# A softmax weighting moved behind the rotated rows of its chunk, and the last layer's norm moved from VectorE to ScalarE, in a two-layer audio tower

## The reference

```
h = layernorm(layernorm(patches(x)) @ W + b)                       # 64 sequences of 23 rows, 512 wide
h = h + power_attention(layernorm(h))                              # layer 0
h = h + shared_expert(layernorm(h)) + top4_of_16_experts(...)
h = h + softmax(rope(Q) rope(K)^T / sqrt(32), causal) V Wo         # layer 1, 16 heads, 4 of keys and values, from layernorm(h)
h = h + down(silu(gate(z)) * up(z)),  z = layernorm(h)
      # gate, up, down: x -> int8 rows of rmsnorm(x) (scale 127 / max|x| per row), ternary weights
```

## Time and profile before

| | |
|---|---|
| median of three runs | 1389.83 us |
| the profiled execution | 1393.95 us, of which its span 1391.8 us |
| TensorE busy | 1228.5 us (88%) |
| VectorE busy | 864.6 us (62%) |
| ScalarE busy | 613.2 us (44%) |
| mean granted TensorE clock | 0.939 of full speed |

### The profile page before, as it was taken

How to read it: one execution, slowest core, us unless ns; L and a number is a source line. 1 busy time by engine, 2 the same in 40 slices (tenths; PEclk the granted TensorE clock), 3 DMA queues, 4 the chain that set the end, 5 groups by cost and what they waited for, 6 DMA issues and landing times.

```text
span 1391.8 us, 30551 instructions
## 1 busy us (share of the span) xinstructions
PE 1228.5 (88%) x10764; PEld 718.6 (52%) x10778; DVE 864.6 (62%) x1767; ACT 613.2 (44%) x1054; POOL 231.8 (17%) x280
## 2 busy tenths in 40 slices
PE   5999899999999999957799999999957885959997
PEld 2447566666666666635344444444524664424443
DVE  5985454655546555488844454554357677778886
ACT  3444444544445444425244444444423332246664
POOL 2220000000000000000123333333258600110000
PEclk9997999999999999986999999999977887989998
DMA  5121452444524435214147767775247700000000
GB/s 196 61 83 49 154 202 109 181 175 162 198 109 181 181 145 210 107 46 185 46 150 251 265 218 279 262 253 183 92 129 135 105 7 2 1 1 16 23 23 27
DMA packets 43277, 180.98 MB, mean 130 GB/s; under 512 B 9172, under 2 KB 10512, under 8 KB 35408
## 3 DMA queue, kind: packets, MB, share of 16 engines
q0 software_dynamic: 19744, 95.41, 20.7%
q1 hardware_dynamic: 20016, 72.15, 14.6%
q10 hardware_dynamic: 3456, 12.58, 2.5%
HBM read 132.39 MB, written 47.73 MB: 129 GB/s over the span
## 4 chain that ended last, share of the span: by engine, by line
PE 52%; DVE 24%; issue 13%; ACT 4%; POOL 2%; DMA 2%; DVEq 1%; another core or an unknown queue 0%; SPq 0%; ACTq 0%; POOLq 0%
PE ps L935 14%; PE ps L937 13%; PE ps L936 13%; DVE rs L1611 2%; PE ps L1049 2%; DVE ff L2043 2%; DVE amf L2050 2%; PE ps L1028 1%; PE ps L1123 1%; PE ps L1376 1%; DVE we_sp L1405 1%; DVE bst L1478 1%; PE ps L1264 1%; ACT vp L682 1%; PE ps L1358 1%
## 5 line engine op out<-in xcount | busy, mean ns | idle before, releaser
L935 PE MATMUL ps<-nT_hi,wa_hi 128*128 128x368 f16 x576 | 189.2, 328 | 11.8 <-DVE wa_lo L1405 7.7
L936 PE MATMUL ps<-nT_lo,wa_hi 128*128 128x368 f16 x576 | 188.8, 328 | 0.0
L937 PE MATMUL ps<-nT_hi,wa_lo 128*128 128x368 f16 x576 | 188.1, 327 | 0.0
L1772 DVE SCALAR_TENSOR_TENSOR nrm<-ps,xg,nrm 128x256 f32<-128x256 f32 x61 | 29.5, 483 | 122.9 <-ACT nrm L749 103.1
L523 POOL DMA_INDIRECT xg<-xrow,idx x61 | 61.2, 1004 | 263.4 <-PE ps L1123 113.8
L935 PE MATMUL ps<-wide,xT 128*128 x244 | 92.7, 380 | 13.8 <-issue 9.3
L1605 DVE SCALAR_TENSOR_TENSOR a<-sq,eps_row,E 128x184 f32<-128x184 f32 x32 | 13.1, 409 | 131.3 <-ACT sq L699 131.3
L1579 DVE SCALAR_TENSOR_TENSOR wide<-ps,wide 128x368 f32<-128x368 f32 x128 | 66.8, 537 | 42.0 <-PE ps L937 42.0
L936 PE MATMUL ps<-wide,xT 128*128 x244 | 92.5, 379 | 0.0
L937 PE MATMUL ps<-wide,xT 128*128 x244 | 92.5, 379 | 0.0
L1358 PE MATMUL ps<-qw,qT 128*128 128x512 bf16 x372 | 85.6, 383 | 4.0 <-DVE ff L2043 2.6
(11 more groups left out here) (317 smaller groups left out, 2893.6 us busy)
## 6 DMA issues: line engine op xcount, KB each, us to landing
we_st<-in_we POOLq DMA_DIRECT2D x16, 1536.0 KB, 6.8
wsp<-we_sp POOLq DMA_DIRECT2D x16, 1536.0 KB, 5.4
wide<-wsp SPq DMA_DIRECT2D x16, 1536.0 KB
yslot<-yt POOLq DMA_DIRECT2D x61, 256.0 KB
wq_st<-in_ffq SPq DMA_DIRECT2D x24, 512.0 KB, 4.5
wq_st<-in_ffq ACTq DMA_DIRECT2D x24, 512.0 KB, 3.5
wide<-in_wa SPq DMA_DIRECT2D x10, 1024.0 KB, 6.9
xt<-in_x SPq DMA_DIRECT2D x12, 512.0 KB, 3.5
```

The costliest lines, as they stand in the source:

```text
L935: nc.tensor.matmul(dst, lhs[0], rhs[0], start=start, stop=False)
L936: nc.tensor.matmul(dst, lhs[0], rhs[1], start=False, stop=False)
L937: return nc.tensor.matmul(dst, lhs[1], rhs[0], start=False, stop=stop)
L1772: V.scalar_tensor_tensor(ht, ps[:, 2 + p, FI:2 * FI], AS / WS if x is None else xgw[:, x, ds(D + e, 1)], sgt[:, p, :], ALU.mult, ALU.mult) ...
```

## The change

1. In chunk c, VectorE does `weights(c-1)` behind all rotations, `rotated(c)` and the low halves of the next rows, just ahead of `centred(c)`. `group_stats(c+1)` goes between `rotate(c, 0)` and `rotate(c, 1)`, `group_shift(c+1)` behind `rotate(c, 1)`, and `low(k)` behind `rotate(c, 3)`.
2. TensorE does `turn(c-1)` behind `project(c+1, 0)` and `(c+1, 1)`, just ahead of `weighted(c-1)`. The two row turns and `scores(c)` follow `project(c, 5)` directly. ScalarE does `weights_turned(c-1)` behind `moved(c+1, 1)`, ahead of `exponential(c)`.
3. The last layer's norm is one ACTIVATE on ScalarE (bias and scale per row, `f_norm`); VectorE only writes the bias (`f_shift`, one column). The turn on VectorE is now `w_add(n)`, `f_shift(n-2)`, `largest(n-3)`, `w_moments(n-1)`, and is written out instead of looped.
4. The first scales are taken of four rows (turns 6 and 7) instead of eight, and the integers of rows 0 and 1 are written in turns 8 and 9, amid the output rows. The scales of the other eight are asked for behind the last row and worked out behind turn 3 of the last pipeline.
5. TensorE does `q_turn(0)` between `out_rows(10)` and `out_rows(11)`; ScalarE does `f_turned_rows(0)` behind the square of row 9; the first `gate_up` waits for all of `w_add`.

```
# POOL
-            pipeline(pool, NT, [(0, lambda k, p, half: root(rf_ask, k, rt_in[:, p:p + 1], rt_out[:, p:p + 1], rf_done))])
-            for n, x in enumerate((slice(0, EARLY), slice(EARLY, NT))):
-                root(rq_ask, n, rq_in[:, x], rq_out[:, x], rq_done)
+            for k in range(NT):
+                if k == FIRST + 2:                                   # FIRST = 4
+                    root(rq_ask, 0, rq_in[:, 0:FIRST], rq_out[:, 0:FIRST], rq_done)
+                root(rf_ask, k, rt_in[:, k % 2:k % 2 + 1], rt_out[:, k % 2:k % 2 + 1], rf_done)
+            root(rq_ask, 1, rq_in[:, FIRST:NT], rq_out[:, FIRST:NT], rq_done)
# ScalarE, attention
                 moved(c, 5)
-                if c:
-                    weights_turned(c - 1)
                 ...
                     moved(c + 1, 0)
                     moved(c + 1, 1)
+                if c:
+                    weights_turned(c - 1)
                 exponential(c)
# ScalarE, rows
+            def f_norm(k):
+                act.wait_ge(w_nb, k + 1)
+                nc.scalar.activation(xn[:, k, :], h[:, k, :], ACT.Identity, bias=nb12[:, k % 2:k % 2 + 1],
+                                     scale=rt_out[:, k % 2:k % 2 + 1]).then_inc(w_n, 1)
-            pipeline(act, NT, [(0, f_square)])
+            for k in range(NT):
+                f_norm(k)
+                f_square(k)
+                if k == NT - 3:
+                    f_turned_rows(0, 0, 0)
# TensorE
-                if c:
-                    turn(c - 1, k if inner else NT - 1)
                 if inner:
-                    for j in (k + 1, k + 2):
-                        pe.wait_ge(f_pe, ready(4 * (c - 1) + 2 + j % 2))
-                        row_turn_l1(j)
+                    row_turn_l1(k + 1)
+                    row_turn_l1(k + 2)
                 ...
                 scores(c)
                 if c + 1 < CH:
                     project(c + 1, 0)
                     project(c + 1, 1)
                 if c:
+                    turn(c - 1, k + 2 if inner else NT - 1)
                     weighted(c - 1)
-            for k in range(NT):
+            for k in range(NT - 1):
                 out_rows(k, k % 2, k // 2)
             def gate_up(k, fs):
                 if fs[0] == 0:
+                    if type(k) is int and k == 0:
+                        pe.wait_ge(w_h, ready(NT - 1))
                     pe.wait_ge(w_ev, k + 2)
                 ...
-                              (1, lambda k, p, half: gate_up(k, (2, 3))), (2, f_turn)])
+                              (1, lambda k, p, half: gate_up(k, (2, 3))), (2, f_turn)],
+                     after={0: lambda: out_rows(NT - 1, (NT - 1) % 2, (NT - 1) // 2)})
# VectorE, attention: the new order
+                rotate(c, 0)
+                if inner: group_stats(c + 1)
+                rotate(c, 1)
                 ...                                                  # y_low(c - 2) as before
+                if inner: group_shift(c + 1)
+                rotate(c, 2); rotate(c, 3)
+                if inner: low(k)
+                rotate(c, 4); rotated(c)
+                if inner: low(k + 1); low(k + 2)
+                if c: weights(c - 1)
                 centred(c)
# VectorE, rows
+            def f_shift(k, p, half):
+                dve.wait_ge(rf_done, k + 1)
+                V.scalar_tensor_tensor(nb12[:, p:p + 1], mv12[:, p, 0:1], -1.0, rt_out[:, p:p + 1], ALU.mult, ALU.mult).then_inc(w_nb, 1)
-            pipeline(dve, NT, [(0, w_add), (2, f_norm), (1, w_moments), (3, largest)], order, 2,
-                     after={NT: lambda: ask_rows(0, EARLY), NT + 1: lambda: row_scales(0, 0, EARLY)})
-            ask_rows(EARLY, NT)
+            for n in range(NT + 3):
+                for lag, step in ((0, w_add), (2, f_shift), (3, largest), (1, w_moments)):
+                    if 0 <= n - lag < NT:
+                        step(n - lag, (n - lag) % 2, 0)
+                if n == FIRST + 2:
+                    ask_rows(0, FIRST)
+                if n == FIRST + 3:
+                    row_scales(0, 0, FIRST)
+                if 0 <= n - NT + 4 < AHEAD:                          # AHEAD = 2
+                    quantize(n - NT + 4, 0, 0)
+                    integers(n - NT + 4, 0, 0)
+            ask_rows(FIRST, NT)
...
-                     order, 1 + 2 + 4 + 2, after={1: lambda: row_scales(1, EARLY, NT)})
+                     order, 1 + 2 + 4 + 2, after={3: lambda: row_scales(1, FIRST, NT)})
```

More of the change, by code:

```diff
@@ L40 @@
 EARLY = 8
+FIRST = 4
+AHEAD = 2
 GT = 3
@@ L363, in build @@
         f_pt, f_pe, f_av, f_hi, f_lo = sems("f", "pt pe av hi lo")
-        w_mm, w_h, w_n, w_sq, w_am, w_r, w_q, w_tr, w_ev = sems("w", "mm h n sq am r q tr ev")
+        w_mm, w_h, w_nb, w_n, w_sq, w_am, w_r, w_q, w_tr, w_ev = sems("w", "mm h nb n sq am r q tr ev")
         x_gu, x_dq, x_sg, x_t, x_sq, x_am, x_q, x_tr, x_ev, x_dn, x_og = sems("x", "gu dq sg t sq am q tr ev dn og")
@@ L867, in _, with f_square @@
             y_high(CH - 1)
-            def f_square(k, p, half):
+            def f_norm(k):
+                act.wait_ge(w_nb, k + 1)
+                nc.scalar.activation(xn[:, k, :], h[:, k, :], ACT.Identity, bias=nb12[:, k % 2:k % 2 + 1],
+                                     scale=rt_out[:, k % 2:k % 2 + 1]).then_inc(w_n, 1)
+            def f_square(k):
                 act.wait_ge(w_n, k + 1)
                 act.wait_ge(w_sq, k + 1)
-                nc.scalar.activation(jk, xn[:, ds(k, 1), :].rearrange("p a b -> p (a b)"), ACT.Square,
-                                     accum_out=Gm["ssq"][:, ds(k, 1)]).then_inc(w_sq, 1)
+                nc.scalar.activation(jk, xn[:, k, :], ACT.Square, accum_out=Gm["ssq"][:, k:k + 1]).then_inc(w_sq, 1)
             def f_turned_rows(k, p, half):
@@ L910, in f_turned, with f_turned_next @@
                                          ps[:, 4 + j, :].bitcast(BF16), ACT.Copy).then_inc(x_ev, 1)
-            pipeline(act, NT, [(0, f_turned_rows), (1, gated), (2, f_turned)])
+            def f_turned_next(k, p, half):
+                if type(k) is not int or k > 0:
+                    f_turned_rows(k, p, half)
+            pipeline(act, NT, [(0, f_turned_next), (1, gated), (2, f_turned)])
         @block.tensor
@@ L1947, in _ @@
                 k = GT * (c + 1)
+                inner = 0 < c < CH - 1
                 rotate(c, 0)
+                if inner:
+                    group_stats(c + 1)
                 rotate(c, 1)
@@ L1955, in _ @@
                     y_low(c - 2)
-                if c:
-                    if c + 1 < CH:
-                        group_stats(c + 1)
-                        group_shift(c + 1)
-                    weights(c - 1)
-                for j in range(2, 5):
-                    rotate(c, j)
-                    if j == 2 and 0 < c < CH - 1:
-                        low(k)
+                if inner:
+                    group_shift(c + 1)
+                rotate(c, 2)
+                rotate(c, 3)
+                if inner:
+                    low(k)
+                rotate(c, 4)
                 rotated(c)
-                if 0 < c < CH - 1:
+                if c == 0:
+                    group_shift(1)
+                    low(k)
+                if inner or c == 0:
                     low(k + 1)
                     low(k + 2)
-                if c == 0:
-                    group_shift(1)
-                    for j in range(GT):
-                        low(k + j)
+                if c:
+                    weights(c - 1)
                 centred(c)
@@ L1990, in w_moments @@
                 ask(mv12[:, p, 1:2], 1.0, 1e-5, rt_in[:, p:p + 1], rf_ask)
-            def f_norm(k, p, half):
+            def f_shift(k, p, half):
                 dve.wait_ge(rf_done, k + 1)
-                V.tensor_scalar(xn[:, ds(k, 1), :].rearrange("p a b -> p (a b)"), row(k), mv12[:, p, 0:1],
-                                rt_out[:, p:p + 1], ALU.subtract, ALU.mult).then_inc(w_n, 1)
+                V.scalar_tensor_tensor(nb12[:, p:p + 1], mv12[:, p, 0:1], -1.0, rt_out[:, p:p + 1], ALU.mult, ALU.mult).then_inc(w_nb, 1)
             def largest(k, p, half):
@@ L2033, in integers, with later @@
                                 ALU.subtract, ALU.min).then_inc(w_q, 1)
+            for n in range(NT + 3):
[10 more added lines that the diff above has]
+            ask_rows(FIRST, NT)
+            def later(step):
+                return lambda k, p, half: step(k, p, half) if type(k) is not int or k >= AHEAD else None
             def dequantizers(k, p, half):
@@ L2076, in finish @@
                                        ALU.add).then_inc(x_og, 1)
-            pipeline(dve, NT, [(0, quantize), (0, integers), (2, dequantizers), (2, product(0)), (2, product(1)),
+            pipeline(dve, NT, [(0, later(quantize)), (0, later(integers)), (2, dequantizers), (2, product(0)), (2, product(1)),
```

(2 more changed lines are left out.)

## The result

The changed kernel takes 1381.94 us (median of five runs, 1376.59 to 1385.54) against 1391.47 us for the kernel before (five runs): a ratio of 0.9943, interval 0.9924 to 0.9961. Beside other kernels later it took 1380.64 us against 1390.51 (0.9936, 0.9910 to 0.9962). So 8 to 10 us were won; 12.5 had been worked out. The profiled execution took 1385.54 us with a span of 1383.3, that is 8.5 us less than the profile of before.

A forecast was written before the change was run, and what follows sets the result against it. TensorE (88% busy) was taken as the bound, with holes from list order and a VectorE chain behind the output rows. Attention 9.0 + rows 3.5 = 12.5 us took the median from 1389.83 to 1377.3 us, range 1371.5 to 1384.

The forecast's parts named there:

- Chunk 1, 1.7 us: Attention, chunk 1: earlier statistics remove TensorE's norm wait (1.2 us); moving the turn of weights gains 0.5.
- Chunk 2, 3.6 us: Attention, chunk 2: earlier statistics gain 1.2 us; the new order of turn and row turns gains 2.4.
- Cost 0.7, counted above: Chunk 2: VectorE stands 1.8 us for POOL's last gathers before row 11's statistics, delaying `qp`; TensorE loses 0.7 us.
- the gathers become the bound: Rival, chunk 2: gathers land 4 us later than counted, moving `qp` and TensorE by 4; 1381.3 us, chance 0.12.
- Chunk 3, 3.0 us: Attention, chunk 3: 3.3 us gained before scores(3), the turn fills TensorE's 3.56 us wait, 0.3 off for its last copy.
- The clock, +0.7 (bounds -3 to +3): Attention: low-clock stretches stay but shift phase; 0.7 us won, as chunk 2's turn now follows projections.
- the 9.0 of the forecast: Whole attention gain: 1.2 + 1.2 + 0.5 + 2.4 + 3.0 + 0.7 = 9.0 us.
- Output rows, 3.6 - 0.8 + 0.7: Rows to gate_up: first Silu 3.6 us sooner, 0.8 off for pieces behind it, 0.7 for table load; 3.5 us, bounds 0.5 to 5.5.
- The 0.7 for a table load ahead of the dequantizers: Behind the output rows: Silu's table load may start before VectorE's dequantizers, 0 to 1.3 us; 0.7 taken.
- The rival "the rows give nothing": Output rows: VectorE's 3.8 us of added work and ScalarE hand-overs eat the tail's gain; 1380.8 us, chance 0.10.
- ScalarE's dearer norm: Output rows: norm costs 0.81 us on ScalarE against 0.54 on VectorE, but only the last row's is on the path.
- the slow rival: TensorE stays at 1.2 GHz from scores(1) until the output rows: +17 us, 1394 us, chance 0.04.

The follow-up runs named there:

- first set of experiments: Four kernels run beside the kernel before on one chip: attention alone, rows part alone, gathers earlier, weights(3) first; 1373.68 to 1390.71 us.
- gathers earlier: Changed kernel with two gathers for rows 9 and 10 issued by POOL ahead of the inverse roots of rows 6 to 8: 1375.77 us, 0.9886 of before.
- attention alone: Kernel before with only points 1 and 2 of the change, output rows as before: 1379.77 us against 1393.55, 0.9892.
- weights(3) first: Changed kernel with VectorE's last-chunk softmax weights ahead of chunk 2's low parts and Wo's low part: 1373.68 us, 0.9857 of before.
- the fixes: Changed kernel with two gathers issued earlier, last chunk's weights first and Silu table loaded early, together: 1365.58 us, 0.9829 of before; again 1368.12 us, 0.9840.
- rows part alone: Kernel before with only points 3 to 5 of the change, attention as before: 1390.71 us, 0.9979 of before.
- early table: Changed kernel with one unused one-column Silu on ScalarE ahead of the last copies of turned weights: 1376.78 us, 0.9901 of before.
- the rows taken back: Kernel with the fixes but points 3 to 5 of the change undone: 1375.31 us, 0.9874, against 1368.12 us, 0.9840, for the fixes in that set.
- second and third sets of experiments: Later kernels beside the kernel before, on two other chips: changed kernel again, early table, and the fixes with variants; 1364.07 to 1403.39 us.

## Why the prediction was right or wrong, point by point

- **Direction and rough size.** Right. 8 to 10 us measured, 12.5 forecast; the 1377.3 us lie 4.6 us under the median. The markers: scores(1) from 1099.0 (forecast near 1101), scores(3) until 1159.6 (1156), first output row 1179.5 (1177), first Silu 43.9 us behind it (44 to 45). scores(3) and the first output row lag by what chunks 2 and 3 lost. One sign of being right did not come: no wait on `nrm` above 0.3 us. It was 1.60 in chunk 2.
- **Chunk 1, 1.7 us.** Too small: the stage to weighted(0) went from 36.4 to 31.5. The wait of 1.22 is gone, as worked out, and 3.1 us came from something the sum had no term for: the values took 3.0 us without the gaps of before (6.1). The clock gave next to nothing: the low stretch behind scores(1) was 3.5 us long instead of 6.5, but the one that reaches over E0 was longer, 8.8 against 9.5 in the stage. Without gaps and clock some 1.7 are left, as forecast, though a wait for `qp` that the sum did not have (1.04) stands ahead of scores(1). In the first set of experiments the gaps are back in part in the new order (values 4.9 to 5.3 us), with stages of 32.3 to 34.5; the longest also had more of the low clock. Whether the new order has a share in the shorter gaps no run shows.
- **Chunk 2, 3.6 us.** Nothing came in the changed kernel's profile (30.5 to 30.7), 3.2 in its repetition, 5.8 where the gathers were out of the way. The term that failed is "Cost 0.7, counted above". The landing was right (1113.4 forecast, statistics of row 11 at 1113.66), but VectorE came to it sooner than I had it, since chunk 1 had gone faster behind the point at which the gathers are issued: it stood 3.2 us in three waits instead of 1.8 in one, and 2.6 us of that reached TensorE (1.60 on `nrm`, which I had as removed, and 0.95 more on `qp` than with the gathers earlier). The rival "the gathers become the bound" had the place right, with another cause: not that they land late, but that all else comes early. scores(2) started at 1126.5 where the forecast has 1126, so what chunk 1 won above its forecast was lost here. Where the values kept much of their gaps (attention alone 5.3 us, weights(3) first 4.9) TensorE had no such wait on `nrm`. Of the 5.8 with the gathers out of the way, 3.4 are the clock. Two readings of the sum were off by little: the wait on `nrm` in chunk 2 of before was 1.43, not 1.22 again, and from the root to the fall of the DMA share it is 21.8 us, not 22.3.
- **Chunk 3, 3.0 us.** 1.0 in the profile, 3.8 in the repetition, 3.9 with the fixes. The order gives what was said. What I missed is that the turn of weights, with scores ahead of it and no projections, always runs cold: 3.4 to 3.8 us in each profile with the new order, 2.6 before.
- **The clock, +0.7 (bounds -3 to +3).** In the changed kernel's profile it was outside the bounds: up to weighted(2) TensorE worked 7 us longer at the lower level than before, which is some 3.6 lost. Scores(2) and (3) at the lower level cost 2.7 and 2.4 us over the kernels where they ran at the higher one. Over the four profiles with this attention and no fix the stretch from E0 to S is 95.6 us, 9.4 under that of before: the 9.0 of the forecast hold as a mean, with executions at 6.2 to 12.7. That it fits so well is in part luck: 2.5 of the 9.4 are the shorter values, which the sum did not have, and they stand in for what the wait on the gathers took.
- **Output rows, 3.6 - 0.8 + 0.7.** The pieces: the first Silu won 4.2 (3.6 forecast). The cold pieces are there in the changed kernel: 5.31 us against 3.63, the 1.7 that I had; with the rows part alone and with the gathers earlier they ran at the full clock. The 0.7 for a table load ahead of the dequantizers did not come: the load stands 0.10 us behind them, as before. S to the end is 201.8 us in the mean of five profiles with the new rows and no early table (199.1 to 203.8), 205.1 in three with the old: 3.3 us, against 3.5. The changed kernel's own profile has 1.2 of them. The rival "the rows give nothing" is refuted by the set with the rows taken back.
- **ScalarE's dearer norm.** Off the path, as argued: ScalarE has 16.9 of 36 us, and in its last turns VectorE waits for it once, 0.28 us at the last maximum.
- **The clock stays at 1.2 GHz**, the slow rival: no profile shows it. What the Trainium skill says in "TensorE: Matmul & The Clock Gate", Part 4, of transposes not counting, doesn't come out here either: turn(0) and turn(1), which now follow two projections, ran at the full clock (2.4 and 2.5 us). turn(2) and turn(3), behind scores and behind the hole, ran at the lower level, and the clock came back within them or in `weighted` behind.
- **What the forecast never asked** was which waits the change leaves. The hole in front of the last turn (8.6 us, in both profiles) is longer than any that it removed, and half of it goes by moving one line.

Not settled: what sets the moment at which the clock falls, what makes the gaps in the values, and why attention alone was as fast as the whole on its chip.

## What to carry to other kernels

When a reordering lets one engine reach a point sooner, look at what else has to be there by then: a transfer that had slack becomes the wait, and it is paid at each reader down the line. A wait also moves the work behind it against the clock's low stretches, so a gain or loss in one profile may be twice its cause or nothing; compare several executions by stages with the same end points before believing either. And price the largest hole that stays beside the ones that a change removes.

## What the runs showed of the hardware that was not expected

- TensorE's granted clock went down to 1.2 GHz in or just behind each of scores(1) to (3) whatever the order (in one profile, the rows part alone, only 8.4 us behind scores(1)), and 15 dense matmuls among each did not hold it: 0.61 to 0.74 in the three scores that had them.
- A dense bf16 matmul of 368 columns between groups of small fp32 matmuls (32 rows) costs 0.37 us (0.61 less 0.24), more than twice the 0.155 us from start to start of the projections' f16 matmuls of 368 columns.
- In all seven profiles without the early Silu, ScalarE loaded Silu's table only when the Silu was released: 0.10 us behind VectorE's dequantizers, 0.46 to 1.00 us after ScalarE had run out of work. Squares, copies and Identity behind an early Silu caused no further load (one load in the hole, none at 1219.58).
- The same 192 small matmuls of chunk 1's values took 2.9 to 3.0 us in the changed kernel's profile and in all eight of the second and third sets of experiments, and, with gaps that no engine ends ("issue"), 4.9 to 5.9 in the four of the first set and 6.1 in the kernel before.
